# A graph layer with 64 experts: own buffers and earlier gathers for the last three pairs, and fewer closing products

## The reference

```
x1  = x + gnn(xn, edges) + mix(xn)          # graph convolution and linear attention
xl  = layernorm(x1)
sel = route(xl)                             # 4 hashes, best 2 of them: 2 of 64 experts for each token
y   = moe(xl, sel, W1, W2)                  # expert e: gelu(buf[e] @ W1[e]) @ W2[e], W1 512x256, W2 256x512
out = x1 + y.mean(over the 2 choices)
```

## Time and profile before

| what | value |
| --- | --- |
| time, median of 3 runs (lowest to highest) | 546.93 us (546.12 to 547.05) |
| the profiled execution's own time | 547.36 us |
| its span | 545.5 us |
| mean granted TensorE clock | 0.996 |
| busy TensorE, VectorE, ScalarE, GpSimd | 97%, 64%, 47%, 17% of the span |
| DMA, read and written | 93.48 and 17.84 MB |

### The profile page before, as it was taken

How to read it: one execution, slowest core, us unless ns; L and a number is a source line. 1 busy time by engine, 2 the same in 40 slices (tenths; PEclk the granted TensorE clock), 3 DMA queues, 4 the chain that set the end, 5 groups by cost and what they waited for, 6 DMA issues and landing times.

```text
span 545.5 us, 8617 instructions
## 1 busy us (share of the span) xinstructions
PE 528.1 (97%) x2858; PEld 368.3 (68%) x2858; DVE 346.7 (64%) x985; ACT 253.9 (47%) x557; POOL 90.7 (17%) x119
## 2 busy tenths in 40 slices
PE   9899999999999999999999999998999999999896
PEld 7344444555599888899999999985555544544455
DVE  6978797889664655458886233497543544354677
ACT  4878487566455443046664221457433333243200
POOL 2304012000000000000000000004344443544210
PEclk9999999999999999999999999998999999999999
DMA  8600000000100009091009213987999999999978
GB/s 309 213 1 2 1 0 2 1 1 1 55 25 1 1 16 364 16 384 62 0 3 354 77 70 106 412 335 230 387 405 414 417 415 410 415 416 416 410 291 315
DMA packets 32426, 105.70 MB, mean 194 GB/s; under 512 B 4656, under 2 KB 10033, under 8 KB 25340
## 3 DMA queue, kind: packets, MB, share of 16 engines
q1 hardware_dynamic: 23852, 88.54, 42.0%
q0 software_dynamic: 4880, 9.78, 4.8%
q10 hardware_dynamic: 3648, 6.80, 3.4%
HBM read 93.48 MB, written 17.84 MB: 204 GB/s over the span
## 4 chain that ended last, share of the span: by engine, by line
PE 71%; DMA 9%; DVE 8%; issue 6%; POOL 2%; ACT 2%; DVEq 1%; ACTq 0%; POOLq 0%
PE PS L538 8%; PE PS L537 8%; PE PS L539 8%; PE PS L626 6%; PE PS L589 4%; PE PS L655 4%; PE PS L656 4%; PE PS L867 4%; PE PS L853 4%; PE PS L578 3%; PE PS L772 3%; DMA XG<-xx_rows,TIDX 3%; DMA BIG<-xx_rows,TIDX 3%; PE PS L615 3%; DMA KSUM<-xx_rows,TIDX 2%
## 5 line engine op out<-in xcount | busy, mean ns | idle before, releaser
L537 PE MATMUL PS<-ROUND 128*128 128x416 f32 (+3 forms) x232 | 83.9, 361 | 0.0
L538 PE MATMUL PS<-ROUND 128*128 128x416 f32 (+3 forms) x232 | 83.6, 360 | 0.0
L539 PE MATMUL PS<-ROUND 128*128 128x416 f32 (+3 forms) x232 | 83.4, 359 | 0.0
L867 PE MATMUL PS<-BIG 128*64 128x512 f32 x208 | 52.9, 593 | 0.2 <-DVE BIG L1293 0.2
L1107 DVE BATCH_NORM_STATS2 BST<-BIG 128x6 f32<-128x416 f32 (+1 forms) x36 | 20.7, 590 | 44.0 <-ACT BIG L1471 35.4
L537 PEld LDWEIGHTS PS<-ROUND 128*128 128x128 f32 (+1 forms) x232 | 43.5, 188 | 2.6
L539 PEld LDWEIGHTS PS<-ROUND 128*128 128x128 f32 (+1 forms) x232 | 43.6, 188 | 2.5
L538 PEld LDWEIGHTS PS<-ROUND 128*128 128x128 f32 (+1 forms) x232 | 43.5, 188 | 2.4
L655 PE MATMUL PS<-ROUND 128*128 128x416 f32 (+3 forms) x120 | 43.7, 364 | 0.0
L656 PE MATMUL PS<-ROUND 128*128 128x416 f32 (+3 forms) x120 | 42.2, 352 | 0.0
L987 DVE TENSOR_SCALAR BIG<-BIG 128x180 f16<-128x180 f16 (+20 forms) x157 | 42.2, 317 | 0.0
(11 more groups left out here) (276 smaller groups left out, 985.3 us busy)
## 6 DMA issues: line engine op xcount, KB each, us to landing
BIG<-in_we SPq DMA_DIRECT2D x46, 1024.0 KB
BIG<-in_we SPq DMA_DIRECT2D x12, 512.0 KB
y_rows<-KVB SPq DMA_DIRECT2D x19, 256.0 KB
BIG<-y_rows SPq DMA_DIRECT2D x9, 512.0 KB, 8.2
EXTRA<-in_we SPq DMA_DIRECT2D x4, 1024.0 KB
XA<-in_we SPq DMA_DIRECT2D x4, 1024.0 KB
BIG<-in_wqkvp SPq DMA_DIRECT2D x3, 1024.0 KB, 10.3
XA<-in_we SPq DMA_DIRECT2D x6, 512.0 KB, 29.3
```

The costliest lines, as they stand in the source:

```text
L537: mm(o, ah, bh, start=first, stop=False)
L538: mm(o, ah, bl, start=False, stop=False)
L539: return mm(o, al, bh, start=False, stop=last)
L867: ins = mm(PS[64 * j:64 * j + 64, b, :], HT[:, s, 128 * f2 + 64 * j:128 * f2 + 64 * j + 64], weights(2 * r + j, 1024 + 512 * f2, 512), sta ...
```

## The change

1. The last three pairs get buffers of their own, `big(2048 + 512 q, 512)`. All three are filled with zeros behind scatter 21. Pair 29 is gathered behind scatter 22 (and gather 28), pairs 30 and 31 behind scatter 23.
2. Pair 29 is both scattered and multiplied. `STEPS` = [6, 10, 10] says for how many tiles a late pair is added by products: pair 29 for tiles 0 to 5, the others for all. Its scatter uses `SCL`, a copy of its index with every row of tiles 0 to 5 moved out of bounds, so that only rows of tiles 6 to 9 are written. Its table `HOT` is 1000 wide instead of 1250. The closing products are 52 instead of 60.
3. ScalarE makes the half `YHI` of pairs 29 and 30, behind the Gelus of pairs 30 and 31; VectorE still makes both parts for pair 31. VectorE's order at the end is written out.
4. `NM2` and the three small operations for `SCL` move to VectorE's place behind pair 24's sum. The third table is built at pair 28 instead of 29.
5. Tile 0 is reloaded as soon as scatter 28 has landed, and its row sum stands on VectorE between the sum and the remainder of pair 30. Tiles 6 to 9 are reloaded after scatter 29 has landed.
6. One semaphore, `s_tail`, counts masked index (1), means (2), tables (3, 4, 5), remainders (6, 8, 9) and tile 0's row sum (7).

```diff
-HOT_AT = {27: (0, 1), 29: (2,)}
+FIRST_OF_LAST = 6
+STEPS = [FIRST_OF_LAST] + [NT] * (LATE - 1)
+HOT_AT = {27: (0, 1), 28: (2,)}
+LATE_GATHERS = {22: (29,), 23: (30, 31)}
...
     order = expert_order()
-    for r in range(32 - LATE, 31):
-        order.remove(("down", r))
-        order.insert(order.index(("hid", r + 1)) + 1, ("down", r))
-    return order
+    order = order[:order.index(("down", 29)) + 1]
+    return order + [("hid", 30), ("split", 29), ("hid", 31), ("down", 30), ("sum", 0), ("split", 30), ("down", 31),
+                    ("split", 31)]
...
+        XG = [XG[r % NB] for r in range(32 - LATE)] + [big(2048 + D * q, D) for q in range(LATE)]
...
TensorE, closing products
+                        begin = min(t for t in range(LATE) if j < STEPS[t])
                         for t in ts:
-                            if t == 0 and j < 8:
+                            if t < begin:
+                                continue
+                            if t == begin and j < 8:
                                 pe.wait_ge(moved[b], use - 1)
...
                             if j == 0:
-                                pe.wait_ge(s_hot, t + 1)
-                                bd, ud = at_of(("down", 32 - LATE + t))
-                                pe.wait_ge(moved[bd], ud)
+                                pe.wait_ge(s_tail, HOTS[t])
+                                pe.wait_ge(s_tail, SPLITS[t])
...
VectorE
+            def row_sum(i, value, signal):
+                n = rows(i)
+                dve.wait_ge(sd_row[i], value)
+                V.scalar_tensor_tensor(YL[0:n, i, 0, :], YL[0:n, i, 0, :], NM2[0:n, i:i + 1], YL[0:n, i, 1, :], ALU.add,
+                                       ALU.add).then_inc(signal, 1)
...
+                    V.tensor_tensor(y, PS[:, b, :], y, ALU.add).then_inc(moved[b], 1)
+                    if r == 30 - 2 * LATE:
+                        link(V.tensor_copy(SCF[:, 0:1], SCIDX[:, 32 - LATE:33 - LATE]))
+                        link(V.tensor_scalar(SCF[:, 1:2], SCF[:, 0:1], 256.0 * FIRST_OF_LAST - 0.5, 8192.0, ALU.is_lt, ALU.mult))
+                        V.tensor_tensor(SCL, SCF[:, 0:1], SCF[:, 1:2], ALU.add).then_inc(s_tail, 1)
+                        dve.wait_ge(s_nm, NT)
+                        V.tensor_scalar(NM2, NM[:, :], -2.0, None, ALU.mult).then_inc(s_tail, 1)
...
+                elif kind == "split":
+                    t, y = r - (32 - LATE), XG[r]
+                    if t < LATE - 1:
+                        dve.wait_ge(s_hi, t + 1)
+                    else:
+                        dve.wait_ge(moved[b], use)
+                        link(V.tensor_scalar(YHI[:, t, :], y, 0.5, None, ALU.mult))
+                    V.scalar_tensor_tensor(YLO[:, t, :], y, 0.5, YHI.bitcast(F32)[:, t, :], ALU.mult,
+                                           ALU.subtract).then_inc(s_tail, 1)
+                elif kind == "sum":
+                    dve.wait_ge(s_tail, MEANS)
+                    row_sum(r, 32, s_tail)
...
ScalarE, behind the Gelu of pair r
+                    if r > 32 - LATE:
+                        bd, ud = at_of(("down", r - 1))
+                        act.wait_ge(moved[bd], ud)
+                        A.activation(YHI[:, r - 33 + LATE, :], XG[r - 1], ACT.Identity, scale=0.5).then_inc(s_hi, 1)
...
GpSimd
-            for r in range(32 - LATE):
+            for r in range(33 - LATE):
                 scatter_pair(r)
                 n = r + LEAD
-                if n < 32:
+                if n < 32 - LATE:
                     if n >= NB:
                         pool.wait_ge(sd_ys[n % NB], 16 * (n // NB))
...
                     gather_pair(n)
+                if r == 21:
+                    for q in range(32 - LATE, 32):
+                        G.memset(XG[q], 0.0).then_inc(s_xz, 1)
+                    pool.wait_ge(s_xz, LATE)
+                for q in LATE_GATHERS.get(r, ()):
+                    gather_pair(q)
...
SyncE
+            for sm, value in stored(sd_ys, 31 - LATE, NB):
+                sp.wait_ge(sm, value)
+            reload(range(1))
             sp.wait_ge(s_res, 1)
...
-            for i in range(NT):
-                n = rows(i)
-                sp.dma_start(YL[0:n, i, :, :], yv[128 * i:128 * i + n, :, :]).then_inc(sd_row[i], 16)
+            for i in range(1, NT):
+                if i == FIRST_OF_LAST:
+                    for sm, value in stored(sd_ys, 32 - LATE, NB):
+                        sp.wait_ge(sm, value)
+                reload(range(i, i + 1))
```

More of the change, by code:

```diff
@@ L436, in gnn_mix_moe @@
         YL = big(20240, 10240).rearrange("p (i a d) -> p i a d", i=NT, a=2)
-        HOT = by(rounded(KK0, 1250 * LATE), LATE)
+        WIDE = [-(-min(128 * t, N) // 250) for t in STEPS]
+        HOT = [rounded(KK0 + 250 * sum(WIDE[:t]), 250 * WIDE[t]) for t in range(LATE)]
         YHI, YLO = (by(rounded(36992 + 512 * LATE * q, 512 * LATE), LATE) for q in range(2))
         LTK, LTQ = big(32800, LATE), by(big(32800 + LATE, 5 * LATE), LATE)
+        SCL, SCF = big(32800 + 6 * LATE, 1).bitcast(I32), big(32801 + 6 * LATE, 2)
         yv = y_d.rearrange("(t a) d -> t a d", a=2)
@@ L479, in gnn_mix_moe @@
         sd_w2 = [sem(f"d_w2{q}") for q in range(2)]
-        sd_w = {n: sem("d_w" + n) for n in "khvqp"}
+        sd_w = {n: sem("d_w" + n) for n in "kvqp"}
         sd_we = [sem(f"d_we{q}") for q in range(NPR)]
@@ L491, in gnn_mix_moe @@
                              "agg", "hth", "htl", "qz", "qzl", "kvt", "mh"))
-        s_hot, s_xz, s_nwt, s_ohv = sem("hot"), sem("xz"), sem("nwt"), sem("ohv")
+        s_tail, s_xz, s_nwt, s_ohv, s_hi = (sem(n) for n in ("tail", "xz", "nwt", "ohv", "hi"))
+        MASKED, MEANS, HOTS, SUMMED, SPLITS, SUMMED_AGAIN = 1, 2, (3, 4, 5), 7, (6, 8, 9), 10
         (s_link, s_w1h, s_w1s, s_w2s, s_nv, s_ns, s_nb, s_relu, s_h1h, s_h1s, s_xst, s_rstd, s_nm, s_sel, s_par, s_lgz, s_ohs, s_lq,
@@ L1286, in vector @@
             for step in eviction_order():
-                kind, r, (b, use) = step[0], step[1], at_of(step)
+                kind, r = step
+                if kind != "sum":
+                    b, use = at_of(("down", r) if kind == "split" else step)
                 if kind == "hid":
@@ L1594, in gather_pair @@
             def gather_pair(r):
-                G.indirect_dma_start(out=XG[r % NB], out_offset=None, in_=xx_d[:, :],
+                G.indirect_dma_start(out=XG[r], out_offset=None, in_=xx_d[:, :],
                                      in_offset=bass.IndirectOffsetOnAxis(ap=TIDX[:, r:r + 1], axis=0),
@@ L1744, in sync, with reload @@
                     load_half(e, h)
+            def reload(tiles):
+                for i in tiles:
+                    n = rows(i)
+                    sp.dma_start(YL[0:n, i, :, :], yv[128 * i:128 * i + n, :, :]).then_inc(sd_row[i], 16)
+            for sm, value in stored(sd_ys, 31 - LATE, NB):
+                sp.wait_ge(sm, value)
+            reload(range(1))
             sp.wait_ge(s_res, 1)
@@ L1748, in sync @@
                 end_of_experts(sp)
+                sp.wait_ge(s_tail, SUMMED)
                 full_sp(sp)
-            for sm, value in stored(sd_ys, 31 - LATE, NB):
-                sp.wait_ge(sm, value)
-            for i in range(NT):
-                n = rows(i)
-                sp.dma_start(YL[0:n, i, :, :], yv[128 * i:128 * i + n, :, :]).then_inc(sd_row[i], 16)
+                reload(range(1))
+            for i in range(1, NT):
+                if i == FIRST_OF_LAST:
+                    for sm, value in stored(sd_ys, 32 - LATE, NB):
+                        sp.wait_ge(sm, value)
+                reload(range(i, i + 1))
         def wide_dve(eng):
```

56 lines of the change are left out of this document (23 added, 33 removed).

## The result

The kernel before has a median of 546.93 us and the changed one of 548.06 us, over 15 runs each. The ratio is 1.0021, with a 95% interval of 1.0012 to 1.0029: 0.2% slower, 1.1 us, and 0.8 us above the top of the range. Three executions in all the runs, of 1370 to 3030 us, are left out of every median and ratio here. So two traces that are read side by side show only 0.2 us of the 1.1; they can say which waits came and went, and the timed runs have to say what each is worth.

The account below looks back on a forecast made before the run. TensorE, busy 97% of the span, was taken as the bound; -1.86 + 0.77 - 0.5 = -1.59, rounded to -1.5 us after giving back 0.1, took the median from 546.93 to 545.4 us, range 544.6 to 547.3.

Parts of the forecast that it names:

- Own buffers and sooner gathers: Expert stage: late pairs' gathers issued sooner, so TensorE's two stalls at pairs 28 and 29 go, -1.86 us.
- the last rival: Expert stage: gathers come no sooner for TensorE or hold up weights; one 0.9 us stall stays, 546.3 us, chance 0.08.
- Four small operations: VectorE after pair 24's sum: they delay pair 25's copy and TensorE with it, +0.77 us.
- The rival with this outcome: After pair 24's sum: small operations cost nothing, total then -2.3 bounded by weights, 544.6 us, chance 0.10.
- Halves on ScalarE: Pairs 29 and 30: halves move to ScalarE at about 0.63 us and fit behind the Gelus, 0.
- Fewer closing products: Closing stage: tiles 6 to 9 drop pair 29's products, VectorE becomes the bound at 1.26 us a tile, -0.5 us.
- The early reload: Tile 0's reload after scatter 28, taken to land in 4.0 us: rows just in time for VectorE's sum, 0.
- the second rival: Tile 0's row sum on VectorE waits for its reloaded rows: 546.3 us, chance 0.27.
- Scatter 29 and the second wait: Reloads 6 to 9 behind scatter 29: covered by slack before the last reload's use, 0, at most +1 us.

Follow-up runs that it names:

- experiment 1: Kernel before with only the last three pairs' own buffers and sooner gathers: 546.46 us, 0.9995 of the kernel before.
- experiment 2: Changed kernel, three separate edits: 60 products without scatter 29's rows or wait, 547.26 us; small operations behind pair 25's copy, 547.85; tile 0's row sum last, 547.17.
- the flag first: Changed kernel with SyncE's wait and read of the overflow flag ahead of the first reload; alone 546.49 us, also combined with other edits.
- Experiment 4: Changed kernel with SyncE's wait and read of the overflow flag moved ahead of the first reload: 546.49 us, 0.9995 of the kernel before.
- experiment 3: Both kernels reloading only the first of each token's two rows: changed 545.48 us (0.9973), before 545.97 us (0.9987).
- experiment 7: 15 expert loads cut by 128 of 2048 columns: kernel before with sooner gathers alone 544.48 us, kernel before 545.25, changed kernel with flag read first 545.71.
- both repairs: Changed kernel's small operations put behind pair 25's copy and tile 0's row sum put last; with flag read first, within 0.1% of the kernel before.

## Why the prediction was wrong, by its steps

**Own buffers and sooner gathers, -1.86.** The first half of the mechanism was right: both stalls went, the gathers stand within 0.7 us of the times forecast (491.33, 494.09, 495.44 against 492.0, 494.6, 496.0: all sooner), and the last hidden transposes came 1.21 us sooner even after what the small operations took. The worth was wrong. Alone it is 0.3 us, not told from nothing. TensorE waits 1.6 us for its weights there (experiment 1), which the last rival had, at a chance of 0.08 and with one stall of 0.9. And of the 1.3 us by which the reloads went out sooner, 0.5 us reached VectorE's last row sum, which had to wait for its rows.

**Four small operations, +0.77.** They took 0.52 us: four starts from 497.79 to 498.31, at 0.18 and 0.08, not 0.20, and the sum ahead of them overlaps the first. In the total they are worth nothing (experiment 2). The rival with this outcome expected a gain from it; there was none, as weights and rows came next.

**Halves on ScalarE, 0.** Right. Each half took 0.63 us, as the squares of the same shape. VectorE waited 0.4 us for that of pair 29 and not at all for that of pair 30 (done at 524.97, wanted behind the row sum that began at 525.07).

**Fewer closing products, -0.5.** TensorE's side was right, 52 products and the last 2.5 us sooner. VectorE was not 1.26 us a tile at the end but as fast as rows came: its last row sums begin 1.90 and 1.65 us apart. With the flag first, 52 products are 0.12% faster than 60 (both with the wait), 0.7 us, with overlapping intervals: the forecast of 0.5 us may be right there, and isn't shown. With the pause the same 8 products fewer brought nothing (1.0021 against 1.0015).

**The early reload, 0.** This is the step that failed, in what it left out. The row sum of tile 0 did wait, 0.77 us, as scatter 28 took 5.3 us and not 4.0; that is the second rival, and putting the sum last brought 0.4 us, with overlapping intervals. I counted the wait of the engine that uses the row and not what SyncE has to do between reload 0 and reload 1. The flag's wait, its reading and the branch lie there now, 522.49 - 521.14 = 1.35 us between two reloads that are otherwise some 0.4 to 0.7 apart, and the 0.86 us by which the first came sooner are gone: the second goes out at 522.49, against 522.3 before. Experiment 4 shows what it cost: without it the changed kernel is 1.4 us faster. Reload 1 alone is held back by less, some 1.0 us (1.35 against the 0.38 between the first two reloads with the flag first), so a delay passed on one for one is not the whole mechanism.

**Scatter 29 and the second wait, 0, at most +1.** It failed with the same error behind it, a cover that was not there. I took the last reload of before to land at 539.0 and to be used at 540.1, 1.1 us to spare. But the 12.3 us on which this rests is the flight of the ninth reload, issued at 526.16: it landed at 538.46 and was used at 538.73. The last one, for which the view has no landing, took 13.4 us, landed at 540.11 and was used at 540.13. So before had 0.3 us to spare at tile 8 and none at the last tile. And I had forecast the reloads 1.4 us sooner where the later ones went out 0.5 us later (527.17 against 526.7). Even so the time of issue alone doesn't set when rows come: with the flag first the last reload goes out 0.6 us later than in the changed kernel and is used at 539.73 instead of 540.89. The second wait itself took 0.3 us in the trace and, with 60 products, 0.02 to 0.06% in the runs; the term was small, and its sign was in the range I gave.

Together: -1.5 had been forecast, +1.1 came. 1.4 of the difference is the pause. The rest, 1.2 us, is what the gathers and the fewer products should have brought and what the kernel with the flag first, at -0.3, does not have: the closing stage moves 5 MB of rows and 2.6 MB of output behind the last weights, and most of TensorE's lead ends there. That the reloaded bytes bound the changed kernel's closing stage is shown by experiment 3, and that fewer weight bytes are worth time by experiment 7. How weights, reloads and output share the loss isn't shown.

The Trainium skill (DMA: Bandwidth & Descriptors, Anatomy of one DMA), by which the 256 KB scatter would have taken 2.6 us as an estimate, is further from this trace than from that of before (3.4 us): scatter 28 took 5.3 us until SyncE went on.

**Open.** Why the pause costs 1.4 us with 52 products and some 0.4 in the kernel before or with 60. And why the DMA engines, 0.89 to 0.94 busy, moved only 285 and 286 GB/s from 524 to 526 us in the changed kernel and in that with 60 products, 264 in the kernel before with the pause, but 377 in the kernel before, 371 with the gathers alone and 398 with the flag first. It goes with the pause in these, but 60 products with the flag first have it too (289), and 52 with the flag first and both repairs lie between (326), so the pause alone doesn't explain it. Each figure is of one execution, and it isn't shown that they differ from kernel to kernel rather than from execution to execution.

## What to carry to other kernels

When a transfer is moved ahead in a queue, list what the queue does between it and the next one: the first came 0.9 us sooner here, and the nine that mattered did not. Before slack at the end is counted, make sure that both times belong to the same transfer: the longest of nine landings was taken for that of the tenth, which had none in the view and took 1.1 us longer, and that was all the slack there seemed to be. And where an engine is 97% busy but the DMA engines are full up to its last stages, test the bytes first (halve a transfer, cut a load), in the kernel before and in the changed one: here that showed an end bound by rows in one (2.6 us) and hardly in the other (0.7 us).

## What the runs showed of the hardware

- A wait of SyncE that is already met, a register read and a branch between two DMA starts took 1.35 us in the changed kernel (521.14 to 522.49) and 1.33 in the kernel before with the pause (521.64 to 522.97), against 0.38 us from one start to the next with nothing between them (521.02 to 521.40 with the flag first). In the kernel before the same read and branch ran from 497.33 to 498.15 us, and SyncE then stood waiting for scatters until 521.89, so there they delayed nothing.
- Scatter 29, with the rows of only four of ten token tiles to write, took GpSimd 1.36 us to issue, against 0.98 for scatters 27 and 28, and 4.71 us until SyncE went on. But scatter 26, with all its rows, took 1.41 us to issue in the same trace, so the masked rows aren't shown to be the reason.
- From 524 to 526 us the DMA engines were 0.94 busy and moved 286 GB/s in the changed kernel, and were 1.01 busy and moved 398 with the flag first.
- Of nine reloads of 512 KB issued within 6 us, the first landed 3.8 us after its issue and the ninth 12.7; VectorE, waiting, went on 0.02 us after the ninth's landing (539.22 and 539.24).
